# Expert weights of an attention and mixture-of-experts block loaded as bfloat16 and widened on ScalarE, with loads and zeroing cut and moved within the batch

## The chip, the cores and the metric

The kernel runs on one core of a Trainium2 chip. The metric is the device time of one launch in microseconds (us); lower is better.

## The reference

The input `x` has 8 batches of 256 tokens with 256 channels. Per batch six modulation vectors come from `silu(c) @ wmod` (`sa, ca, ga, sb, cb, gb`; the two gates are kept at least 0.25 away from zero).

```python
h = _layernorm(x) * (1 + ca) + sa
x = x + ga * attention(h)      # 32 heads of 8 channels, window of 8 keys each way
h = _layernorm(x) * (1 + cb) + sb
x = x + gb * experts(h)
```

`attention` multiplies the scores in the window by a triangular factor, takes a softmax over the window, and projects with `proj_w` and `proj_b`. `experts` sends each of the 2048 tokens to 2 of 16 experts by its sigmoid scores (float32), each expert being `(silu(h w1) * (h w3)) w2` with 176 hidden channels; a shared expert with 352 hidden channels is added for every token. The expert weights (`w1`, `w2`, `w3`, `sw1`, `sw2`, `sw3`) are bfloat16 arrays; the rest is float32.

## The kernel before, in words

The program is written engine by engine, with a semaphore for each hand-over. It has three stages.

**Stage one, attention, batch by batch.** A batch has two tiles of 128 tokens (`U` = 2). Every engine has a `main(it, first, after)` which `over(main)` calls for `it` = 0 to 7. TensorE, in the order of its own text: turn the normalised x of batch it+1 (`turn_x`), scores of the second tile (`scores(it, 1)`, L1200 and L1210), q of the next batch (`make_q`, L1172), turn the scores back (`turn_p(it, 0)`, L1219), k of the next batch (`make_k`), sums and values of the first tile (`times_v(it, 0)`, L1230 and L1237), `turn_p(it, 1)`, v of the next batch (`make_v`, L1190), the projection (`project`, L1250 and L1252), `times_v(it, 1)`, the first scores of the next batch (`scores(it + 1, 0)`), then `turn_h`, `project(it, 1)` and `gate` for the expert stage's input of the batch before. A float32 matmul has two matmul records and two weight-load records. `times_v` has 128 + 128 short records at L1237, and `scores` 64 + 64 at L1210.

ScalarE (ACT) takes the projections out of PSUM (`scaled_h` L532, `keep_q` L539, `keep_k` L546, `keep_v` L551), does the exponentials (`exponent`, L570, once per tile), and copies for the gate (`turned_h`, `gate_exp`). VectorE (DVE) masks, transposes, takes maxima off, divides by the sums, adds the residual and does both layer norms; in the last two batches it also routes the first ten tiles of tokens (`chances`, `pick`, `ranked`, `placed`). GpSimd (POOL) does the inverse roots (`rstd1`, `rstd2`) and `modulated(b)`, which writes the expert stage's input `hx` of batch b, called in `main` of batch b+1.

Transfers: q and v of each batch are spread out by DMAs. SP (SyncE) issues, per batch, `spread_q` (L352), `values_out` (v to the DRAM tensor `vd`, L358), `modulation` (the vectors of a batch, broadcast to all partitions, L372; it waits for `l2_h`), `values_in` (v back into a block pattern, rows of 256 bytes, L366; it waits for the write and for `times_v` of the batch before) and `load_x(b + 3)` (L335), in this order. `times_v(it + 1, 0)` waits for `values_in`. Everything that SP issues stays in this order.

Within this stage the weights of stage three come in, and the token table of the experts (`hslots`, 47 tiles of 128 rows, 6 MB) is zeroed. ACT issues one sixth of the zeroing (`ZEROED` = 6, 1024 KB, L589) at the end of each of its first six `main`s, and in `main(1)` also the first half of the up weights (`staged`, bfloat16, 1408 KB, L592). POOL issues the shared weights in `main(1)` (`load_shared`, L438 and L439) and the down weights `w2` in `main(2)` and `main(3)` (`load_second`, L443, two DMAs each): these go from bfloat16 in DRAM to float32 tiles in SBUF, the conversion being done by the DMA. POOL's `main` runs ahead of the others: it is in `main(1)` while TensorE is still in batch 0.

**Stage two** is the routing of the rest, and the shared expert for the first half of the tokens. POOL scatters the rows of `hx` into `hslots` (L471) once `row_z` says that the zeroing has ended. **Stage three** runs 47 tiles of rows through their experts (L1377, L1394, L1402, L1409), scatters the results (L506), and adds the rest of the shared expert and the residual.

Before all of this, ACT issues its own loads (L516 to L525) and then `scaled_h(0)` and `keep_q(0)`; half of the q spreading of batch 0 is on ACT's queue (L599). `pads` counts POOL's clearing of tiles; its seventh is after L435.

## Time and profile before

| | |
|---|---|
| median of 3 runs | 432.62 us (428.88 to 434.42) |
| the profiled execution, its own time | 430.5 us |
| its span, first to last instruction | 428.6 us |
| mean granted TensorE clock | 0.948 of full speed |
| busy: TensorE matmul, weight loads | 370.0 us (86%), 278.0 us (65%) |
| busy: VectorE | 310.4 us (72%) |
| busy: ScalarE, GpSimd | 125.5 us (29%), 124.1 us (29%) |
| moved by DMA | 52.45 MB in 53067 packets |

All rows are of that one profiled execution; times in it start at the first instruction. PE is TensorE's matmuls, PEld its weight loads, and a name with q at the end (SPq, ACTq) is an engine's issuing of DMAs. "issue" as the releaser of an idle stretch means that the profile shows no semaphore of another engine for it. The DMA share is the mean busy share of the 16 DMA engines; it is put together from packet times and can exceed 1.

### The profile page before, as it was taken

The page shows a single profiled execution, that of the slowest core. Times are in us where ns is not written, and L with a number is a line of the kernel's source. Part 1 is how long each engine was busy: PE and PEld are TensorE (multiplying, and loading weights), DVE is VectorE, ACT ScalarE, POOL GpSimd, SP SyncE. Part 2 cuts the span into 40 slices and gives each one's busy share as a digit, 9 for nine tenths or more (in the row PEclk, how much of TensorE's full clock was granted, in tenths as well). Part 3 has the DMA queues.
Part 4 walks back from the last instruction along what each step waited for, and adds up shares of the span by engine and source line. Part 5 has one row for each costly group of instructions (what it writes and reads, how often), then busy time and mean ns, then how long its engine had stood idle before and what let it go on. Part 6 is the DMA issues. An engine that isn't in the chain of part 4 may idle for free.

```text
span 428.6 us, 11940 instructions
## 1 busy us (share of the span) xinstructions
PE 370.0 (86%) x4834; PEld 278.0 (65%) x4834; DVE 310.4 (72%) x609; ACT 125.5 (29%) x301; POOL 124.1 (29%) x131
## 2 busy tenths in 40 slices
PE   6889699796999999986686958599999999999962
PEld 3568488685878888865543436477777777764452
DVE  2678578865799999999858496576666667631576
ACT  1123022311213232321023100255555555532520
POOL 6201004040030303030357586024444444440000
PEclk9999789989899999999895988899999999999988
DMA  8163905959354554425012612233333332103923
GB/s 290 54 155 107 249 21 135 263 193 227 114 125 141 106 155 106 133 71 148 2 63 98 220 62 87 77 108 104 119 120 103 114 122 72 41 3 96 297 74 122
DMA packets 53067, 52.45 MB, mean 122 GB/s; under 512 B 22148, under 2 KB 48045, under 8 KB 52406
## 3 DMA queue, kind: packets, MB, share of 16 engines
q1 hardware_dynamic: 40784, 28.68, 25.7%
q0 software_dynamic: 4528, 12.40, 9.1%
q10 hardware_dynamic: 7702, 10.62, 7.3%
q8 instruction: 39, 0.64, 0.7%
q14 instruction: 14, 0.11, 0.1%
HBM read 28.75 MB, written 20.79 MB: 116 GB/s over the span
## 4 chain that ended last, share of the span: by engine, by line
PE 65%; DVE 15%; issue 11%; DMA 2%; POOL 2%; ACT 1%; ACTq 0%; SPq 0%; DVEq 0%; POOLq 0%
PE bank L1394 10%; PE bank L1409 10%; PE bank L1283 7%; PE bank L1210 6%; PE bank L1237 6%; PE bank L1172 5%; PE bank L1346 4%; PE bank L1219 3%; PE bank L1190 3%; PE bank L1402 2%; PE bank L1377 2%; DMA first_region<-wmod 2%; DVE region L746 2%; PE bank L1252 2%; PE bank L1230 2%
## 5 line engine op out<-in xcount | busy, mean ns | idle before, releaser
L506 POOL DMA_INDIRECT yrows<-second_region,sloti x47 | 46.2, 984 | 77.0 <-ACT second_region L639 77.0
L1409 PE MATMUL bank<-w,second_region 88*128 x188 | 48.5, 380 | 0.6 <-DVE second_region L1042 0.6
L1394 PE MATMUL bank<-first_region,second_region 128*128 x141 | 42.8, 313 | 3.8 <-DVE second_region L1032 2.4
L453 POOL TENSOR_TENSOR rstd2s<-ve,cft 128x2 f32<-128x2 f32 x8 | 5.7, 708 | 137.3 <-DVE ve L793 137.3
L1283 PE MATMUL bank<-xT_region,sw 128*128 128x512 f32 (+1 forms) x96 | 45.1, 626 | 0.0
L1394 PE MATMUL bank<-region,second_region 128*128 x141 | 42.7, 312 | 0.0
L1210 PE MATMUL bank<-region,second_region 64*32 64x128 f32 x1024 | 34.5, 283 | 7.3 <-issue 7.3
L471 POOL DMA_INDIRECT hslots<-hx,posi x32 | 35.6, 1111 | 16.1 <-issue 9.0
L1210 PEld LDWEIGHTS bank<-region,second_region 64*32 64x32 f32 x1024 | 28.7, 111 | 15.6 <-issue 15.3
L1237 PE MATMUL bank<-region 128*32 128x16 f32 x2048 | 34.9, 213 | 1.8 <-issue 1.8
L1237 PEld LDWEIGHTS bank<-region 128*32 128x32 f32 x2048 | 34.9, 159 | 2.0 <-issue 2.0
L1346 PE MATMUL bank<-sw,second_region 128*128 128x256 f32 (+1 forms) x96 | 26.1, 432 | 10.2 <-DVE second_region L991 5.8
L1409 PEld LDWEIGHTS bank<-w,second_region 88*128 88x128 f32 x188 | 32.1, 190 | 4.0 <-issue 1.3
L1172 PE MATMUL bank<-second_region 128*128 128x256 f32 x128 | 32.0, 395 | 1.2 <-ACT second_region L532 1.2
L1283 PEld LDWEIGHTS bank<-xT_region,sw 128*128 128x128 f32 (+1 forms) x96 | 17.9, 191 | 22.8 <-issue 22.7
L1346 PEld LDWEIGHTS bank<-sw,second_region 128*128 128x128 f32 (+1 forms) x96 | 20.7, 220 | 16.2 <-DVE second_region L991 6.6
L746 DVE TENSOR_TENSOR region<-bank,cft 128x1024 f32<-128x1024 f32 x16 | 19.5, 1221 | 15.0 <-PE bank L1210 14.9
L769 DVE RECIPROCAL second_region<-bank 128x256 f32<-128x256 f32 x16 | 28.0, 1752 | 2.8 <-PE bank L1230 2.6
L1042 DVE COPY second_region<-bank 88x256 f32<-88x256 f32 x47 | 19.8, 420 | 12.8 <-PE bank L1402 12.7
L1037 DVE TENSOR_TENSOR second_region<-second_region,bank 128x176 f32<-128x176 f32 x47 | 15.9, 338 | 17.9 <-ACT second_region L625 17.9
L1172 PEld LDWEIGHTS bank<-second_region 128*128 128x128 f32 x128 | 23.9, 196 | 6.0 <-issue 3.2
L570 ACT ACTIVATE region<-bank 128x1024 f32<-128x1024 f32 x16 | 16.4, 1023 | 36.2 <-PE bank L1219 36.2
(163 smaller groups left out, 667.1 us busy)
## 6 DMA issues: line engine op xcount, KB each, us to landing
second_region<-hslots SPq DMA_DIRECT2D x47, 128.0 KB, 2.0
hslots<-zeros ACTq DMA_DIRECT2D x5, 1024.0 KB, 6.4
region<-vd SPq DMA_DIRECT2D x32, 128.0 KB, 5.1
region<-yrows SPq DMA_DIRECT2D x16, 256.0 KB, 6.1
modb<-moddram SPq DMA_DIRECT2D x8, 384.0 KB, 5.0
w<-w2T POOLq DMA_DIRECT2D x4, 704.0 KB, 9.1
xs<-x SPq DMA_DIRECT2D x8, 256.0 KB, 6.8
vd<-second_region SPq DMA_DIRECT2D x8, 256.0 KB, 2.2
```

Of the source, the lines that this page charges most:

```text
L471: gp.indirect_dma_start(hslots, bass.IndirectOffsetOnAxis(ap=posi[:, 0, k * TT + t:k * TT + t + 1], axis=0), hx[:, t, :], None).then_inc(r ...
L506: gp.indirect_dma_start(yrows, bass.IndirectOffsetOnAxis(ap=sloti[:, s:s + 1], axis=0), yo[:, s % RING, :], None, bounds_check=TOPK * T - ...
L746: dve.tensor_tensor(S[:, u].rearrange("p g (m t) -> p (g m) t", t=QB), SP[u][:, :].rearrange("p (m t) -> p m t", t=QB), window.unsqueeze(1 ...
L769: dve.reciprocal(rsum[:, u], SM[u]).then_inc(z_r, 1)
L1042: dve.tensor_copy(hT2[0:IH, s % 2], HT(s)).then_inc(ht_s, 1)
L1172: last = pe.matmul(o[:, c * N:(c + 1) * N], wqkv[:, k, off + c * P:off + (c + 1) * P], hT[:, k, :], start=k == 0, stop=k == C - 1)
L1210: last = pe.matmul(SPV[u][KB * o:KB * (o + 1), b // 2, :, b % 2, :], kT[OC * s:OC * (s + 1), c, q0:q0 + KB], qbd[OC * s:OC * (s + 1), c, : ...
L1237: last = pe.matmul(ZP[u][KB * r:KB * (r + 1), c, b * QB:(b + 1) * QB], vbd_h[:, BL * u + b, :, h], PT[:, u, b // 2 * 2 + h % 2, KB * (h // ...
L1283: last = pe.matmul(o[0:p], sw13[:, c, half * SI + f * P:half * SI + f * P + p], xT[:, c, g * GT * P:(g + 1) * GT * P], start=c == 0, stop= ...
L1346: last = pe.matmul(YP(i), hid_g[0:p, g % 2, f, i * P:(i + 1) * P], sw2[0:p, f, :], start=f == 0, stop=f == SK - 1)
L1394: last = pe.matmul(UP(s), parts[:, s % 2, m, c * P:(c + 1) * P], w13[c][:, bass.ds(experts[s], 1), :], start=m == c == 0, stop=m == EXACT ...
L1409: last = pe.matmul(YP(s), hT2[0:IH, s % 2, k, :], w2[:, k, bass.ds(experts[s], 1), :], start=k == 0, stop=k == 1)
```

## The change

- The shared weights and the down weights come as bfloat16, by ACT's queue, into memory that is free at the time: the rows of `hx` for batches 1 to 3 (`sw13_came`, `sw2_came`), the second half of `w2` (`w2_came[0]`) and the rows of `hx` for batches 4 to 7 (`w2_came[1]`). The first three are issued before `scaled_h(0)`, behind a wait for `pads` 7, together with the first eighth of the zeroing; the fourth is issued in `main(0)`.
- ACT widens them in 11 pieces (`piece`): two of 704 columns, one of 768, eight of 1024 columns on 88 partitions. `PIECES` gives each batch its pieces: the first stands between `scaled_h` and `keep_q`, the second between `keep_k` and `exponent(it, 1)`. Each counts `wide_s` up.
- Who writes `hx` of batch b now waits for the pieces that read it (`STAGED`), and TensorE waits for `wide_s` where it waited for the loads.
- The zeroing is in eight parts of 752 KB or less, one before the batches, and one in each of `main(0)` to `main(6)`, right behind `exponent(it, 0)`.
- `staged` is loaded in two halves, in `main(1)` and `main(2)`, behind `exponent(it, 1)`.
- On SP, `load_x(b + 3)` is issued behind `values_out(b + 1)` and ahead of `modulation(b + 1)`.
- POOL issues no weight loads any more.

```diff
-ZEROED = 6
+ZEROED = B
+PIECE = 1024
+PIECES = ((), (0, 1), (2, 3), (4, 5), (6, 7), (8, 9), (10,), ())
...
+        came = hx[:, U:].rearrange("p t d -> p (t d)").bitcast(BF16)
+        sw13_came = came[:, 0:C * 2 * SI].rearrange("p (c i) -> p c i", c=C)
+        sw2_came = came[:, C * 2 * SI:C * 2 * SI + SK * D]
+        w2_came = [w2[:, 1].rearrange("p e d -> p (e d)").bitcast(BF16)[:, 0:E * D],
+                   hx[0:IH, TT // 2:].rearrange("p t d -> p (t d)").bitcast(BF16)]
+        STAGED = {1: 3, 4: 8, 5: 9, 6: 10, 7: 11}
...
                     values_out(b + 1)
+                if b + 3 < B:
+                    load_x(b + 3)
+                if b + 1 < B:
                     modulation(b + 1)
                     values_in(b + 1)
-                if b + 3 < B:
-                    load_x(b + 3)
...
-            def load_shared():
-                gp.dma_start(sw13[:, :, :], sw13T).then_inc(ld_sw, 16)
-                gp.dma_start(sw2[:, :, :], sw2T).then_inc(ld_sw, 16)
-            def load_second(k):
-                for e in range(0, E, E // 2):
-                    gp.dma_start(w2[:, k, e:e + E // 2, :], w2T[:, k, e:e + E // 2, :]).then_inc(ld_w2, 16)
...
                 wait(gp, mod_ld, 16 * (b + 1))
+                if b in STAGED:
+                    gp.wait_ge(wide_s, STAGED[b])
...
+            def zero(k):
+                a, z = k * NS // ZEROED, (k + 1) * NS // ZEROED
+                act.dma_start(hslots_t[:, a:z], zeros[:, :].unsqueeze(1).to_broadcast([P, z - a, D])).then_inc(row_z, 16)
+            def load_second(k):
+                act.dma_start(w2_came[k], w2T[:, k].rearrange("p e d -> p (e d)")).then_inc(ld_w2[k], 16)
+            def load_first(k):
+                n = STAGE // 2
+                act.dma_start(staged[:, k * n:(k + 1) * n], w13T[:, k * n:(k + 1) * n]).then_inc(ld_ew, 16)
+            def piece(i):
+                if i < C:
+                    act.wait_ge(ld_sw, 32)
+                    last = act.activation(sw13[:, i], sw13_came[:, i], ACT.Copy)
+                elif i == C:
+                    last = act.activation(sw2[:, :, :].rearrange("p f d -> p (f d)"), sw2_came, ACT.Copy)
+                else:
+                    k, j = divmod(i - C - 1, E * D // PIECE)
+                    act.wait_ge(ld_w2[k], 16)
+                    at = slice(j * PIECE, (j + 1) * PIECE)
+                    if k == 1:
+                        act.wait_ge(wide_s, C + 1 + E * D // PIECE)
+                    last = act.activation(w2[:, k].rearrange("p e d -> p (e d)")[:, at], w2_came[k][:, at], ACT.Copy)
+                last.then_inc(wide_s, 1)
             def main(it, first, after):
                 if after:
                     scaled_h(it + 1)
+                if PIECES[it]:
+                    piece(PIECES[it][0])
+                if after:
                     keep_q(it + 1)
                 exponent(it, 0)
+                if it == 0:
+                    load_second(1)
+                if it + 1 < ZEROED:
+                    zero(it + 1)
                 if after:
                     keep_k(it + 1)
+                for i in PIECES[it][1:]:
+                    piece(i)
                 exponent(it, 1)
+                if it == 1:
+                    act.wait_ge(mod_p, 3)
+                if it in (1, 2):
+                    load_first(it - 1)
                 if after:
                     keep_v(it + 1)
...
+            act.wait_ge(pads, 7)
+            act.dma_start(sw13_came, sw13T).then_inc(ld_sw, 16)
+            act.dma_start(sw2_came, sw2T.rearrange("p f d -> p (f d)")).then_inc(ld_sw, 16)
+            load_second(0)
+            zero(0)
             scaled_h(0)
             keep_q(0)
```

## Rows read from the trace of the kernel before

**Rows 1.** The page's first part: busy time of each engine.

```profile
PE 370.0 (86%) x4834; PEld 278.0 (65%) x4834; DVE 310.4 (72%) x609; ACT 125.5 (29%) x301; POOL 124.1 (29%) x131
```

**Rows 2.** Chain that ended last, whole span: start, length, what.

```profile
129.68 1.88 PE bank L1210 x64
...
151.22 1.88 PE bank L1210 x64
```

**Rows 3.** The same chain from 38 to 130 us, small pieces too.

```profile
45.06 2.91 issue
...
52.42 3.57 PE bank L1210 x64
...
63.51 0.29 issue
...
82.18 1.35 issue
...
84.52 1.19 issue
...
94.91 0.65 issue
...
102.81 3.76 issue
...
108.42 3.00 PE bank L1172 x8
...
123.68 0.61 issue
```

**Rows 4.** Windows from the span's start: length, busy (xrecords) by engine, clock, DMA.

```profile
0.00:45.06 45.06, 38.19 (x601) 27.27 (x602) 28.59 (x60) 9.06 (x14) 12.31 (x21) 1.00 0.52 158
0.00:61.00 61.00, 50.35 (x734) 36.34 (x736) 38.99 (x70) 12.14 (x19) 12.31 (x21) 0.94 0.54 152
0.00:63.60 63.60, 52.87 (x855) 38.70 (x856) 41.27 (x73) 12.30 (x19) 12.31 (x21) 0.95 0.52 147
...
0.00:102.85 102.85, 88.40 (x1616) 68.35 (x1617) 73.02 (x125) 21.51 (x36) 22.63 (x33) 0.95 0.63 168
```

**Rows 5.** Windows of busy DMA; the last three figures are clock, DMA share, GB/s.

```profile
40.00:54.00 14.00, 10.22 (x255) 7.51 (x257) 9.04 (x12) 1.02 (x2) 1.49 (x3) 0.83 1.00 251
72.00:90.00 18.00, 15.31 (x273) 13.21 (x266) 14.33 (x20) 4.62 (x9) 0.71 (x1) 0.91 1.10 280
98.00:109.50 11.50, 7.60 (x106) 5.78 (x99) 6.59 (x7) 1.88 (x5) 0.00 (x0) 0.90 1.17 252
124.00:132.00 8.00, 7.59 (x146) 6.30 (x146) 7.29 (x9) 1.88 (x5) 0.00 (x0) 1.00 1.00 254
```

**Rows 6.** A window of 2 us in which only large pieces move.

```profile
84.00:86.00 2.00, 0.81 (x54) 0.77 (x46) 1.76 (x1) 0.00 (x0) 0.00 (x0) 1.00 1.09 409
```

**Rows 7.** Timeline of DMA issues: start, length, engine, line, what.

```profile
39.40 0.41 ACTq L589 DMA_DIRECT2D hslots<-zeros  x1
...
40.12 0.78 POOL L438 DMA_DIRECT2D sw<-sw13T  x1
...
69.88 3.25 SPq L366 DMA_DIRECT2D region<-vd  x4
```

**Rows 8.** Timeline of ACT within batch 4; in brackets its idle time before.

```profile
133.52 0.60 ACT L539 ACTIVATE second_region<-bank 128x512 f32<-128x512 f32 x1 [3.49 <-PE bank L1172]
...
139.67 1.02 ACT L570 ACTIVATE region<-bank 128x1024 f32<-128x1024 f32 x1 [2.95 <-PE bank L1219]
```

**Rows 9.** Timeline of the start.

```profile
12.35 0.12 POOL L435 MEMSET apart<- 128x16 f32 x1
...
15.44 1.02 ACT L532 ACTIVATE second_region<-bank,modT 128x256 f32<-128x256 f32 x2 [11.65 <-PE bank L1164]
```

**Rows 10.** Windows of the start and of the change from batch 6 to 7.

```profile
12.00:20.00 8.00, 6.80 (x30) 4.05 (x29) 5.81 (x19) 1.61 (x3) 1.18 (x7) 1.00 0.03 8
...
190.00:212.00 22.00, 14.01 (x387) 11.75 (x383) 20.36 (x37) 2.90 (x5) 1.50 (x2) 0.94 0.35 92
```

More of the change, by code:

```diff
@@ L277, in build @@
         xT_p, xT_s, lg_p, lg_s = (sem(n) for n in ("xT_p", "xT_s", "lg_p", "lg_s"))
-        ld_g, ld_sw, ld_w2, ld_ew, ld_late = (sem(n) for n in ("ld_g", "ld_sw", "ld_w2", "ld_ew", "ld_late"))
+        ld_g, ld_sw, ld_ew, ld_late = (sem(n) for n in ("ld_g", "ld_sw", "ld_ew", "ld_late"))
         su_p, su_s, su_m, sy_p, sy_s, sh_s = (sem("s" + n) for n in ("u_p", "u_s", "u_m", "y_p", "y_s", "h_s"))
@@ L283, in build @@
         row_z = sem("row_z")
+        wide_s = sem("wide_s")
+        ld_w2 = [sem(f"ld_w2{k}") for k in range(2)]
         val_s, slot_p, who_s, exp_s = (sem(n) for n in ("val_s", "slot_p", "who_s", "exp_s"))
@@ L474, in main @@
             def main(it, first, after):
-                if it == 1:
-                    load_shared()
-                elif it in (2, 3):
-                    load_second(it - 2)
                 if not first:
@@ L584, in main @@
                     gate_exp(it - 1)
-                if it == 0:
-                    act.wait_ge(pads, 7)
-                if it < ZEROED:
-                    a, z = it * NS // ZEROED, (it + 1) * NS // ZEROED
-                    act.dma_start(hslots_t[:, a:z], zeros[:, :].unsqueeze(1).to_broadcast([P, z - a, D])).then_inc(row_z, 16)
-                if it == 1:
-                    act.wait_ge(mod_p, 3)
-                    act.dma_start(staged, w13T[:, 0:STAGE]).then_inc(ld_ew, 16)
+            act.wait_ge(pads, 7)
[3 more added lines that the diff above has]
+            zero(0)
             scaled_h(0)
@@ L909, in modulated @@
                 dve.wait_ge(mod_ld, 16 * (b + 1))
+                dve.wait_ge(wide_s, STAGED[b])
                 dve.tensor_tensor(h2[:, :, :], h2[:, :, :],
@@ L1322, in main @@
                 if not after:
-                    pe.wait_ge(ld_sw, 32)
+                    pe.wait_ge(wide_s, C + 1)
                     pe.wait_ge(ga_s, TT - 1)
@@ L1413, in _ @@
             pe.wait_ge(su_m, SK * AHEAD)
-            pe.wait_ge(ld_ew, 16)
+            pe.wait_ge(ld_ew, 32)
             pe.wait_ge(ld_late, 16)
-            pe.wait_ge(ld_w2, 64)
+            pe.wait_ge(wide_s, 11)
             pe.wait_ge(exp_s, 1)
```

## The prediction

> **What bounds the kernel now.** I read the page's busy times first: TensorE's matmuls are 86% of the span and no other engine passes 72% [rows 1]. So the end is set by TensorE and by whatever stops it. The chain that ended last tells what stops it. Where nothing does, a batch of the attention takes 151.22 - 129.68 = 21.54 us from one run of second scores to the next [rows 2]. The three batches before that took 129.68 - 52.42 = 77.26 us [rows 2, 3], which is 12.6 us over 3 x 21.54.
>
> The small pieces of the chain show where it goes: seven stretches called "issue", of 2.91, 0.29, 1.35, 1.19, 0.65, 3.76 and 0.61 us, together 10.8 us [rows 3]. The stretches of 2.91 and 3.76 us lie in the middle of 64 matmuls of one loop, which have no semaphore between them, so no other engine's work is awaited. Counting records shows what is. Up to the first stretch TensorE has 601 + 602 = 1203 of them, up to the second 855 + 856 = 1711, up to that at 102.81 us 1616 + 1617 = 3233 [rows 4]. The distances are 508 = 2 x 254 and 1522 = 6 x 253.7. I read this as blocks of about 254 visible instructions, fetched from memory while the block before them is run; TensorE stands when the next one isn't there.
>
> The Trainium skill, Runtime: NRT & Kernel Launch, section "Instruction fetch mechanics", says that a program is streamed in blocks of 16 KiB, 256 instructions, by a DMA queue of the sequencer's own, while the current one runs, and that crossing a boundary is mostly hidden. The block agrees with the distances above, the hiding does not agree with 3.76 us. By its rule that crossings cost next to nothing these pieces would have another cause and the time would stay; that is a rival below.
>
> How long a fetch takes can be seen twice. With the DMA engines nearly idle, the block that begins just before 61.0 us (734 + 736 = 1470 records, 13 beyond an edge at 1457) [rows 4] is run through by 63.51 us and its successor is there at 63.80 [rows 3]: about 2.9 us. With 14 us of DMA at share 1.00 around it the gap at 45.06 lasts to 47.97, and in the 11.5 us at 1.17 the one at 102.81 lasts to 106.57 [rows 3, 5]. A batch with 8 us at 1.00, from 124 to 132 us [rows 5], has 0.61 us at its beginning, and none of any size later. So what costs is the long stretches. They are long where POOL's converting weight loads meet the zeroing and the values, as at 39.40 and 40.12 us [rows 7], or the load of 1408 KB in batch 1.
>
> The stretch of 1.35 us at 82.18 us is another thing: it stands before `times_v`, which waits for the values that SP issued from 69.88 to 73.13 us [rows 7]. I take it for their late landing, in the stretch 72 to 90 us [rows 5].
>
> After the longer gaps the clock is granted at 1.2 instead of 2.4 GHz for a while: 64 score matmuls take 3.57 us, against 1.88 [rows 2, 3], and the mean clock of the stretch 40 to 54 is 0.83 [rows 5]. All of it beside the gaps is about 12.6 - 7.9 = 4.7 us in batches 1 to 3 (7.85 being the six gaps behind 52.42 us), of which some 0.3 is waiting in the normal order; I take 4.4 us for the clock in all.
>
> **The change part by part.** The sum is made against the profiled execution, 430.5 us, of which the span is 428.6; the median of the runs is 432.6, 2.1 us higher.
>
> *What is removed.* Everything above: gaps of 10.8 us and slow clock of 4.4 us, together 15.2 us, if no stretch of busy DMA stays long. The weights now need half the bytes at their destination, none is converted on the way, and none meets the end of a batch except half of the up weights. POOL loses its issues (0.78 us for one [rows 7]), hidden before and after.
>
> *What is added to the middle of each batch.* Behind `exponent(it, 0)` come 752 KB of zeroing. At the 0.4 MB/us of a window with large pieces [rows 6] this is 1.9 us; in batch 0, with the fourth load of 704 KB, 3.7 us. Just then TensorE comes to `times_v`, 256 records in 2.1 us, where it needs a block in hardly more than the 2.9 us that a fetch takes unhindered. A batch has 972 records (2 x 132 for scores, 2 x 288 for `times_v`, 48 for q, k and v, 84 for the rest), 3.8 blocks, so the edges move through it by some 45 records a batch, and only some batches fall badly. Two short blocks matter. The one around `times_v(it, 0)` falls badly in batch 1 (the gap of 0.29 us): its fetch would be asked for at 61 us, with the zeroing of that batch just begun. The one around `times_v(it, 1)` and the next scores falls badly in batches 0, 2, 3 and 4: there the write of v, the load of x (256 KB, now ahead of the modulation, 0.6 us) and in batch 2 half of the up weights (704 KB, 1.8 us) are before it, in batch 0 also the modulation (384 KB, 1.0 us).
>
> How much of such a backlog a fetch waits for is not in the trace as such. Bounds: none of it, as the gaps of 0.29 to 0.65 us without load show; or all of it. The gap at 45.06 lies between: of 1024 + 704 KB and more issued before it, at 0.4 MB/us over 4.3 us, it saw some 3.3 beyond 2.9. I take three quarters. That gives 0.9 us in batch 0, 0.3 + 1.4 in batch 1, 0.6 + 1.2 in batch 2, 0.6 + 0.4 in batch 3, 0.1 in batch 4: 5.5 us that stay. With none of it 1.6 us stay (0.29 + 0.65 + 0.61), with all of it 7.3. Gaps under 2 us I take to leave the clock alone, as the one of 0.61 did.
>
> *ACT's pieces.* Each first piece stands before `keep_q`, where ACT was idle for 3.49 us, each second one before `exponent(it, 1)`, with 2.95 us [rows 8]. A copy of 1024 columns isn't shown; the nearest row is an exponential of 1024 columns out of PSUM, 1.02 us [rows 8]. Between 0.6 us (512 columns) and twice 1.02 us everything fits into those idle stretches, so I take 0 for all eleven. Were the cover gone, each would cost its 1 us. TensorE's `make_q` runs while the first piece does, so `keep_q` isn't late. Each issue of a DMA on ACT, 0.4 to 0.6 us [rows 7], comes where ACT waits for TensorE anyway (0.7 us or more); I take 0, at most 0.2 each where two meet. The waits for `wide_s` in POOL are met one batch ahead, save that for batch 1, where the third piece comes at the start of batch 2 and the use in its second half.
>
> *The start.* ACT waits for the seventh `pads` at 12.47 us and issues four DMAs, some 2 us, and then has `scaled_h(0)`, for which it sat until 15.44 us [rows 9]. So 1 us is left. The four carry 2.0 MB, 5 us of DMA, into 8 us where the share was 0.03 [rows 10]; ACT's half of the q spreading at 19.3 us comes behind them. They should be through at 18 us. I take 0.3 us; bounds 0 and 2.
>
> *The order on SP.* `load_x` was held up behind the values, and no one waited for it; ahead of `modulation` it puts 0.6 us in front of modulation and values, which have 5 us or more to spare. 0 us beyond the share taken above.
>
> *What is late next.* From the sixth batch on VectorE is busy for 20.4 of 22 us [rows 10]; its work there starts when TensorE lets it and moves forward whole. The expert stage and the zeroing's end (last part near 180 us, awaited by the scatter behind 212) are not on the path.
>
> Sum: 430.5 - 15.2 + 5.5 + 0.3 = 421.1; I round to 421.
>
> **The rivals.**
> - *All stretches short enough.* If a fetch waits for hardly any backlog, 1.6 us stay in place of 5.5: 417 us. For it: 8 us at share 1.00 brought no gap inside the stretch. Against it: batches 0 to 3 had their edges elsewhere.
> - *Middle and end both hurt.* The 752 KB hit every `times_v(it, 0)`, and gaps of 1.5 to 2 us come in six batches, with the clock once or twice: 11 us stay, 427 us. For it: the blocks there are the fastest. Against: in most batches the edge lies outside them.
> - *The middle becomes worse than the end was.* One mechanism: the fetch asked for in `times_v` waits for the whole backlog in all seven batches that have one (3 us each), TensorE stands long enough for the lower clock each time (1 us), 28 us in place of 15.2: 443 us. It decides from 2.2 us a batch. Against it, the same as above, and that 1.9 us of zeroing can hardly cost 3.
> - *The gaps aren't due to transfers.* Then they stay, and the time with them: 430.5 us. Against it: all large ones lie in the stretches of [rows 5].
>
> **How the numbers follow.** Forecast 0.48, all short 0.22, both hurt 0.19, worse than before 0.05, no connection 0.06. The range takes in the first three with the start's bound: 413 to 430. A difference of 2%, 8.7 us, is about what a measurement of this kernel can tell; the border is at 424.0. Faster by over 2%: nearly all of the first two, some of the third, 0.69. Within 2%: 0.26. Slower by over 2%: 0.05.
>
> **What would show it.** In the profile after: seven batches of 21.5 to 23.5 us; no "issue" piece over 2 us in the chain before 190 us, and those that are left at multiples of 254 records, in or right behind `times_v`; no window of 8 us with a DMA share over 1; a granted clock of 1.00 until 190 us. The forecast is wrong if batch 1 to 3 still take 25 us, if gaps sit in the middle of each batch, if `scaled_h(0)` or the first scores come over 1 us later than before, or if ACT's pieces take over 2 us and `exponent(it, 1)` moves.

## The result, and the profile after

| | before | after |
|---|---|---|
| median of 20 runs each | 433.11 us (428.88 to 436.73) | 429.41 us (425.67 to 434.93) |
| ratio, 95% interval | | 0.9915 (0.9887 to 0.9943) |
| the profiled execution, its own time | 430.5 us | 427.58 us |
| its span, clock | 428.6 us, 0.948 | 425.6 us, 0.944 |

The kernel became faster by 3.7 us, where 9.4 were forecast: the right side, inside the range, but well under half of the size, and not more than the 2% by which the text counts a kernel as faster. A kernel's runs can fall into a faster and a slower group; the ratios compare the faster runs alone, the medians are of all runs.

One figure of the change differs from what is said above. The zeroing goes in whole tiles of 128 KB, so its eight parts are 640 KB (the first) and 768 KB (the others), not 752 KB. In the kernel before, the first of the six parts is 896 KB and the others are 1024 KB.

The page of the kernel after, busy time of each engine:

```profile
PE 371.0 (87%) x4834; PEld 278.0 (65%) x4834; DVE 310.1 (73%) x609; ACT 135.0 (32%) x312; POOL 120.7 (28%) x125
```

TensorE's busy time is that of [rows 1]. ACT has 11 instructions and 9.5 us more, which are the pieces; POOL has 6 instructions less. So the work is as described, and the question is again where TensorE stands.

The chain that ended last, kernel after, from 38 to 140 us (start, length, what):

```profile
46.92 0.40 issue
...
51.36 1.88 PE bank L1253 x64
...
60.76 1.91 issue
62.67 0.71 PE bank L1262 x5
63.38 3.02 PE bank L1233 x8
...
66.61 1.16 PE bank L1295 x4
...
76.33 1.88 PE bank L1253 x64
...
91.39 1.20 issue
...
99.05 1.88 PE bank L1253 x64
...
115.12 0.44 issue
...
120.95 1.88 PE bank L1253 x64
...
137.66 0.62 issue
```

Five gaps are left, 0.40 + 1.91 + 1.20 + 0.44 + 0.62 = 4.6 us, where [rows 3] had seven with 10.8 us. From one run of second scores to the next the batches take 25.0, 22.7 and 21.9 us. Batch 1 is the bad one: the gap of 1.91 us splits eight transposes (L1262) into 3 and 5, and behind it the values of the next batch (`make_v`, L1233) take 3.02 us in place of the 1.73 us of the other batches, the projection (L1295) 1.16 in place of 0.86.

Windows of the kernel after (length, busy by engine with records, then clock, DMA share and GB/s); the first three end at gaps:

```profile
0.00:46.92 46.92, 40.19 (x601) 27.77 (x602) 28.76 (x60) 9.06 (x14) 11.00 (x19) 0.96 0.76 215
0.00:60.76 60.76, 52.13 (x855) 37.62 (x856) 41.27 (x73) 13.66 (x21) 11.00 (x19) 0.97 0.68 190
0.00:137.66 137.66, 125.07 (x2506) 98.74 (x2507) 108.12 (x179) 37.88 (x59) 27.29 (x35) 0.98 0.56 155
64.00:66.00 2.00, 2.00 (x6) 1.50 (x5) 0.00 (x0) 0.44 (x1) 1.92 (x2) 0.50 0.73 189
12.00:14.00 2.00, 2.00 (x8) 0.68 (x7) 0.70 (x3) 0.00 (x0) 1.23 (x7) 0.62 0.36 59
```

The first two gaps stand at exactly the records of [rows 4], 601 + 602 and 855 + 856, although the times and everything that the DMAs do there have changed. The last is at 5013 records, 3810 behind the first, 15 x 254. So a gap looks like a block of the program that hasn't come.

The trace shows the block itself. The page's list of DMA queues (packets, MB, share of the 16 engines) has one for instructions:

```profile
q8 instruction: 39, 0.64, 0.6%
```

Each of these 39 packets is of 16384 bytes, and the trace keeps the time of each, though no view prints it. At the gap of 60.76 us the packet runs from 60.18 to 61.06 us, and TensorE goes on at 62.67. At the longest gap of the kernel before it runs from 103.82 to 105.06 us, and TensorE goes on at 106.57. In all 20 profiles of this case the attention has 76 gaps of over 0.25 us at such an edge, and every one ends 0.9 to 1.6 us after the end of such a packet. What waits behind the data is the packet: in `weights_only`, an experiment below that has no burst ahead of this edge, it starts as TensorE enters the block before (57.62 and 57.74 us), in the kernel after 2.0 us later (60.18 and 58.17 us). One gap of the kernel before is of another kind: that at 82.18 us stands at 2388 records, at no edge, before `times_v`.

The rest of the time lies outside the attention's middle. From the first scores (24.17 us before, 26.03 after, in TensorE's timeline) to the second scores of batch 5 (151.14 and 143.08 us) the kernel after gains 9.9 us. Of this it has 2.9 us left at the end. The timeline of TensorE, kernel after, at the start and at the change from batch 6 to 7 (start, length, line, count, idle before):

```profile
11.12 2.30 PE L1189 MATMUL bank<-first_region,cts 128*8 128x512 f32 x4 [2.06 <-DMA first_region<-wmod]
...
190.14 3.50 PE L1253 MATMUL bank<-region,second_region 64*32 64x128 f32 x64
```

The start loses 1.9 us before the first scores, and here the new transfers have no part in it. TensorE waits 2.06 us for `wmod` where it waited 1.63 us, and that wait is over at 11.12 us, before ACT issues its first load of the change (12.54 us); from then on the clock is 0.62 in the window from 12 us. For the spreading of q it waits no longer than before (1.57 and 1.63 us). The profiles of the same kernel and of the kernel before on another chip run the start at full speed. The scores of the last batch take 3.50 us at 1.2 GHz (1.95 in the profile before, but 3.64 in a second profile of the kernel before), which I don't put down to the change either. The clock is down some instructions earlier already, so from the scores before to the end of these the kernel after takes 13.5 us and the kernel before 10.8: 2.7 us. The third piece is new. VectorE and ScalarE, kernel after, timeline of stage two, idle time and its releaser in brackets:

```profile
235.91 0.69 DVE L1030 TENSOR_TENSOR second_region<-second_region,bank 128x512 f32<-128x512 f32 x1 [2.75 <-issue]
239.62 0.26 DVE L881 TENSOR_TENSOR score<-bank,have 128x96 f32<-128x96 f32 x1 [3.02 <-remote]
...
239.71 0.60 ACT L651 ACTIVATE second_region<-bank 128x512 f32<-128x512 f32 x1 [3.83 <-PE bank L1326]
```

The second ranking (`ranked`, L881) follows the line before it in 0.6 us in the kernel before; here it comes 3.02 us late. What it reads from TensorE was written at 235.5 us, and ACT goes on at the same moment. The profile names "remote", on a program of one core, so nothing that it knows. This one lies on the path: the scatter's indices and the tiles' experts come out of this ranking.

### The profile page after: what moved, and what is told of

It reads as the page before. It is cut to its first block, busy times and chain, and to the rows that moved or that the text cites. A ratio compares the mean times of both kernels' runs of the same rounds, so it can differ in the third digit from the quotient of the medians.

```text
span 425.6 us, 11956 instructions
## 1 busy us (share of the span) xinstructions
PE 371.0 (87%) x4834; PEld 278.0 (65%) x4834; DVE 310.1 (73%) x609; ACT 135.0 (32%) x312; POOL 120.7 (28%) x125
## 2 busy tenths in 40 slices
DMA packets 52993, 50.45 MB, mean 119 GB/s; under 512 B 22122, under 2 KB 48147, under 8 KB 52636
## 3 DMA queue, kind: packets, MB, share of 16 engines
q1 hardware_dynamic: 40784, 28.68, 24.5%
## 4 chain that ended last, share of the span: by engine, by line
PE 62%; DVE 17%; issue 12%; DMA 3%; POOL 2%; ACT 1%; another core or an unknown queue 1%; ACTq 0%; SPq 0%; DVEq 0%; POOLq 0%
PE bank L1437 10%; PE bank L1452 10%; PE bank L1280 6%; PE bank L1215 5%; PE bank L1253 5%; PE bank L1326 5%; PE bank L1389 4%; PE bank L1262 3%; PE bank L1233 3%; PE bank L1445 2%; PE bank L1420 2%; DMA first_region<-wmod 2%; DVE region L788 2%; PE bank L1295 2%; PE bank L1273 2%
## 5 line engine op out<-in xcount | busy, mean ns | idle before, releaser
L1253 PE MATMUL bank<-region,second_region 64*32 64x128 f32 x1024 | 33.6, 279 | 1.5 <-issue 1.5
L1326 PEld LDWEIGHTS bank<-xT_region,sw 128*128 128x128 f32 (+1 forms) x96 | 17.9, 191 | 22.8 <-issue 22.7
L1215 PE MATMUL bank<-second_region 128*128 128x256 f32 x128 | 30.9, 385 | 1.2 <-ACT second_region L537 1.2
L672 ACT ACTIVATE second_region<-bank 128x256 bf16<-128x256 f32 x47 | 18.0, 383 | 29.4 <-PE bank L1420 29.3
```

The source lines that it names most:

```text
L672: act.activation(parts[:, s % 2, 0], RTP(s), ACT.Copy).then_inc(hi_s, 1)
L1215: last = pe.matmul(o[:, c * N:(c + 1) * N], wqkv[:, k, off + c * P:off + (c + 1) * P], hT[:, k, :], start=k == 0, stop=k == C - 1)
L1253: last = pe.matmul(SPV[u][KB * o:KB * (o + 1), b // 2, :, b % 2, :], kT[OC * s:OC * (s + 1), c, q0:q0 + KB], qbd[OC * s:OC * (s + 1), c, : ...
L1326: last = pe.matmul(o[0:p], sw13[:, c, half * SI + f * P:half * SI + f * P + p], xT[:, c, g * GT * P:(g + 1) * GT * P], start=c == 0, stop= ...
```

## The experiments

Eighteen kernels ran in five groups, four of them repeats. Each group ran on one chip, and its kernels share the runs of the kernel before; ratios are to those, with their 95% intervals, and times are compared within a group first.

**First group: the kernel itself again, and two of its parts.**

> The changed kernel once more, to see which pieces of its profile come back. Theory A (what the attention gains is given back behind it, by the program itself): the wait of 3.0 us before the second ranking (L881) and the slow clock between batches 6 and 7 (64 score matmuls in 3.5 us) are there again, and the scatter of the first round starts about 6 us earlier than before. Theory B (the losses behind the attention are chance of one execution): at least one of the two is gone and the execution is 2 to 5 us shorter. Both expect gaps of 4 to 6 us in the attention in place of 10.8.

> The kernel before once more. Theory A: no wait before its second ranking, full clock between batches 6 and 7, gaps of 9 to 12 us in the attention. Theory B: the gaps of the attention are there, and one of the two losses behind it may show here as well.

424.77 us against 429.32 before, 0.9909 (0.9868 to 0.995): the result repeats. The profile has gaps of 1.64, 0.94, 0.44 and 0.61 us and no wait at L881. The second profile of the kernel before, 429.53 us, has gaps of 2.36, 2.54, 0.98, 1.13, 3.29 and 0.70 us, 11.0 in all; the largest is again in the second scores of batch 3 (102.18 us), and the one of 2.54 us, at 78.95 us, is new in size. It stands before `times_v`, as that of 82.18 us did.

`late_load` moves the late up weights (`w13_late`, into the memory of the first modulation weights) behind more of ACT's work:

```diff
+            for n in range(3, SK * AHEAD - 1):
+                silu_g(n)
             act.wait_ge(z_p, TT)
             act.dma_start(w13_late, w13T[:, STAGE:]).then_inc(ld_late, 16)
-            for n in range(3, SK * AHEAD):
-                silu_g(n)
+            silu_g(SK * AHEAD - 1)
```

> The late half of the up weights (w13_late, 1408 KB) is issued behind the fifth silu of the shared expert instead of behind the third, some 7 to 10 us later. If the wait of 3.0 us before L881 is an instruction block of VectorE held up by this load, it goes, and the time is 2 to 3 us under the changed kernel's (ratio to before about 0.985), unless the load holds up another block in its new place. If the wait has another cause, it stays and the time with it (0.991).

423.14 us, 0.9907 (0.9865 to 0.9949), the same as `after_again`. On this chip neither kernel has the wait, so it says nothing of it. The two profiles differ in one thing that matters below: behind nearly the same gap in batch 1, 1.64 and 1.65 us, `after_again` has `make_v` at 2.64 us, a slow clock, and `late_load` at 1.73, full speed.

`zero_end` leaves the first part of the zeroing where it is and takes the seven others from the middle of the batches to their ends:

```diff
-                if it + 1 < ZEROED:
-                    zero(it + 1)
...
                     gate_exp(it - 1)
+                if it + 1 < ZEROED:
+                    zero(it + 1)
```

> The changed kernel with the eight parts of the zeroing (but the first) put back to the end of each batch. If the burst in mid-batch causes the gap of 1.91 us in batch 1 behind times_v, that gap falls to about 0.3 us; the gaps at the end of batches 2 to 4 grow or stay. Theory that placement matters: the attention changes by more than 2 us, ratio 0.98 or 1.0. Theory that only size and conversion matter: within 1 us of the changed kernel, 0.99.

423.07 us, 0.9893 (0.9829 to 0.9956). Batch 1's gap is down to 0.26 us; one of 1.55 us is in batch 0. By time alone the kernel can't be told from `after_again` (1.7 us less) or `late_load` (0.1 us less), the interval being 1.3% wide, but the gap went when the burst left the middle.

**Second group: one part of the change alone.** `weights_only` is the kernel before with the weights as bfloat16, ACT's pieces and the waits for them; the zeroing stays in six parts at the ends of batches, the up weights are issued together in batch 1, SP's order is the old one. `zero_only` is the kernel before with the eight parts (one ahead, seven mid-batch), `x_only` has only `load_x` moved. `x_undone` is the kernel after with SP's old order:

```diff
-                if b + 3 < B:
-                    load_x(b + 3)
-                if b + 1 < B:
                     modulation(b + 1)
                     values_in(b + 1)
+                if b + 3 < B:
+                    load_x(b + 3)
```

> The kernel before with only the weights changed: bfloat16 by ACT's queue into free memory and widened by ACT; zeroing in six parts at the ends of batches, the up weights in one stretch in batch 1, and SP's order, all as before. Theory C (the long stretches came from the converting loads): the gaps of 2.9 and 3.8 us at the ends of batches 0 and 2 shrink below 1.5 us, those of batch 1 (up weights and zeroing together) stay; attention 5 us shorter than before, the ratio 0.993. Rival (size of the zeroing parts decides): attention less than 2 us shorter, ratio 1.0.

> The kernel before with only the zeroing changed: eight parts, the first ahead of the batches, the others behind the first exponential of batches 0 to 6. Theory C: the gaps at the ends of batches 0 and 2 stay above 2 us because the converting loads are there, and batch 1 gains a gap of 1.5 us behind times_v; ratio 0.997 to 1.003. Rival (size of the zeroing decides): attention 5 us or more shorter, ratio 0.993.

> The kernel before with only SP's order changed (load of x ahead of modulation and values). All theories: no gap goes, within 1 us of before, ratio 1.00. If the load of x in front of a block asked for in times_v costs what I took (0.4 to 0.9 us in batches 0 and 2 to 4), the attention is 0.5 to 2 us longer.

> The changed kernel with SP's order put back. If the load of x costs the gaps of batches 2 to 4, they shrink by 0.3 us each and the ratio to before is 0.989; if it frees the values, ratio 0.993. I expect no difference that can be measured: 0.991.

| kernel | median, us | ratio to before (429.19 us) |
|---|---|---|
| `weights_only` | 418.51 | 0.9746 (0.9674 to 0.9818) |
| `zero_only` | 430.68 | 1.0037 (0.998 to 1.0095) |
| `x_only` | 430.27 | 1.0011 (0.9969 to 1.0052) |
| `x_undone` | 423.39 | 0.9888 (0.9816 to 0.9961) |

The weights alone give 10.7 us, where the whole change gave 3.7 above and, without SP's order (`x_undone`), 5.8 us here. That is far more than the 0.993 expected: the gaps put down to batch 1's loads were to stay and went too. (The gap at 45 us, on the other hand, stays above the 1.5 us expected.) The other two parts alone can't be told from nothing (1.5 and 1.1 us over the kernel before, with 1.0 inside both intervals). The chain of `weights_only` from 38 to 140 us has two gaps left of the seven:

```profile
45.07 1.82 issue
...
110.19 0.41 issue
```

And that of `zero_only`, same stretch, has six, of which five are shown (the last is 0.32 us):

```profile
44.92 2.89 issue
...
61.26 1.91 issue
...
77.09 1.40 issue
...
84.96 1.27 issue
...
107.68 1.67 issue
```

The reader is to see three things. With the converting loads on POOL's queue the gap at 45 us (2.9) stays wherever the zeroing is. The largest gap of [rows 3], 3.76 us at 102.81 us and 3233 records, is not there: these scores run through. What stands at 107.68 us is at 3360 records, at no edge, and so is that at 84.96; both are before `times_v`, of the kind of the gap at 82.18 us in [rows 3]. So moving the zeroing took away a gap of the end of batch 2 that was expected to stay, and gained others, and the time can't be told from that of the kernel before. And a gap of 1.91 us at 61.26 us appears that is only 0.29 us in [rows 3]: it is the kernel after's gap at 60.76 us, made by the zeroing in the middle of batch 1 without any help of the weights.

**Third group: each small part on top of `weights_only`.** `w_zero_mid` has the eight parts of the zeroing as in the kernel after; `w_zero_start` has the first of the six parts ahead of the batches and the others at their ends; `w_halves` has the up weights in halves behind `exponent(it, 1)`; `w_x` has SP's new order.

```diff
-                if it < ZEROED:
+                if 0 < it < ZEROED:
                     zero(it)
...
             load_second(0)
+            zero(0)
             scaled_h(0)
```

> weights_only (ratio 0.9746) with the zeroing of the change added: eight parts, the first ahead of the batches, the others in mid-batch. Theory D (the zeroing's place and cut give back what the weights gain): first scores 0.5 us later, a gap of 1 to 2 us behind times_v in batch 1, and in the medians most of the 5 to 6 us between weights_only and the changed kernel: ratio 0.985 to 0.99. Rival (the other edits do it): ratio 0.975 to 0.98.

> weights_only with the first of its six zeroing parts (1024 KB) ahead of the batches in place of the end of batch 0. If the backlog at the end of batch 0 makes the gap of 1.8 us at 45 us, it falls below 0.5 us; the q spreading of ACT's queue lands 0.5 to 1 us later. Both together: within 1 us of weights_only, ratio 0.973 to 0.977. If what stands at the start costs more than the profile shows, 0.98 or more.

> weights_only with the up weights in two halves, in batches 1 and 2 behind the second exponential. Theory D: no difference, 0.975. Rival (the half in front of the write of v delays a block in batch 2, and the values): a gap of 1 to 2 us in batch 2, ratio 0.98 or more.

> weights_only with the load of x ahead of modulation and values on SP. Theory D: no difference that can be measured, 0.975 to 0.977. Rival: 0.5 to 1 us more of gaps in batches 2 to 4, 0.98.

| kernel | median, us | ratio to before (434.31 us) |
|---|---|---|
| `w_zero_mid` | 427.58 | 0.9876 (0.9821 to 0.993) |
| `w_zero_start` | 424.06 | 0.9783 (0.9718 to 0.9847) |
| `w_halves` | 423.02 | 0.9786 (0.9727 to 0.9846) |
| `w_x` | 423.18 | 0.976 (0.9699 to 0.9821) |

SP's order and the halves have ratios that can't be told from `weights_only`'s. Nor can that of the part ahead of the batches: the runs of `w_zero_start` go from 422.18 to 429.60 us, those of `w_x` from 421.70 to 428.61. Its own expectation missed in two places, the gap at the end of batch 0 being 1.32 us and not under 0.5, and the q spreading over 2 us late. The zeroing in the middle costs 3.5 us against `w_zero_start` and 4.4 against `w_x`. (The part moved by `w_zero_start` is 896 KB, not 1024.) How the start can lose is in the timeline of TensorE; first `w_x`, nothing of the zeroing ahead:

```profile
23.29 0.59 PE L1242 MATMUL bank<-cbt 128*128 128x512 bf16 x2 [1.62 <-DMA region<-second_region]
23.81 1.95 PE L1252 MATMUL bank<-region,second_region 64*32 64x128 f32 x64
```

then `w_zero_mid`:

```profile
25.53 0.62 PE L1242 MATMUL bank<-cbt 128*128 128x512 bf16 x2 [3.69 <-DMA region<-second_region]
26.09 3.53 PE L1252 MATMUL bank<-region,second_region 64*32 64x128 f32 x64
```

TensorE waits for the spreading of q, which is behind 1.9 MB of weights and zeroing, for 3.69 in place of 1.62 us, and then has the scores at half the clock. Both kernels issue that spreading at nearly the same time (19.1 us in `w_zero_mid`, 18.9 in `w_x`). On this chip `w_zero_start` waits for 3.88 us too; the kernels of the first two groups with the same loads ahead wait for 2.0 to 2.5 us.

Batch 1 of `w_zero_mid` has the gap in the middle and no slow clock behind it:

```profile
63.33 1.90 issue
65.23 0.71 PE bank L1261 x5
65.94 1.73 PE bank L1232 x8
```

All four profiles of this group have the wait at the second ranking, 2.3 to 3.0 us.

**Fourth group: no part ahead of the batches, and the load behind the fifth silu.** `no_start_part` is the kernel after with seven parts, in the middle of batches 0 to 6; they are larger, 896 KB in batch 1. `weights_again` is `weights_only` unchanged; `w_late` is it with the edit of `late_load`; `before_third` is the kernel before.

```diff
-ZEROED = B
+ZEROED = B - 1
...
-                if it + 1 < ZEROED:
-                    zero(it + 1)
+                if it < ZEROED:
+                    zero(it)
...
             load_second(0)
-            zero(0)
             scaled_h(0)
```

> The changed kernel with seven zeroing parts, one in the middle of each of batches 0 to 6, and none ahead of the batches. Theory E (the start costs 1 to 4 us, the mid-batch parts the rest): q spreading of batch 0 lands in 1.9 us, first scores at 24.0 us and not later, the gap of 1.6 to 1.9 us in batch 1 stays; ratio 0.980 to 0.986, between weights_only (0.975) and the changed kernel (0.991). If the ratio is that of weights_only, the start was all of it; if that of the changed kernel, the middle is.

> weights_only once more: ratio 0.972 to 0.980. If this chip is one where the wait before the second ranking shows, it is there (2 to 3 us) and the ratio is at the upper end.

> weights_only with the late up weights issued behind the fifth silu of the shared expert. If the load holds up VectorE before the second ranking on this chip, weights_again has the wait and this kernel has none there, and is 2 to 3 us shorter unless the load holds up something behind it; if weights_again has no such wait, both are the same within 0.5%.

> The kernel before: if the wait before the second ranking comes from the load and the chip alone, it shows here as soon as weights_again shows it; if it needs the changed program, it does not.

| kernel | median, us | ratio to before (432.75 us) |
|---|---|---|
| `no_start_part` | 428.77 | 0.9984 (0.9942 to 1.0026) |
| `weights_again` | 423.04 | 0.9847 (0.9785 to 0.9909) |
| `w_late` | 423.32 | 0.9855 (0.9792 to 0.9917) |
| `before_third` | 432.04 | one run |

`no_start_part` was a miss: without the part ahead the first scores are back at 24.16 us, and batch 0 has no gap over 0.2 us any more, yet the kernel isn't better. Chain of waits of `no_start_part`:

```profile
49.25 1.88 PE bank L1252 x64
...
58.66 2.19 issue
60.86 1.23 PE bank L1261 x5
62.08 2.79 PE bank L1232 x8
```

and of `weights_again`, with the zeroing at the ends:

```profile
50.61 1.88 PE bank L1251 x64
...
60.02 0.01 issue
60.03 0.71 PE bank L1260 x5
60.73 1.73 PE bank L1231 x8
```

The block edge is in the same place in both, between the third and the fourth of eight transposes. With 896 KB in front of it it costs 2.19 us, and 0.5 + 1.1 us more by the slow clock in the next two lines; without, 0.01 us. So `no_start_part` takes 25.2 us for batch 1 and `weights_again` 21.4.

The wait of the ranking is longest here, 3.75 us in the chain of `weights_again`:

```profile
228.52 3.75 another core or an unknown queue
...
232.30 0.27 DVE score L879
```

The same kernel in the second group has nothing there:

```profile
229.62 0.69 DVE second_region L1028
230.31 0.18 DVE score L879
```

`w_late` was to take it away if the load issued at that time made it; it has 3.79 us. That explanation is out. `before_third` is the one profile of the kernel before in a group where the wait shows. VectorE's ranking (L839) follows at once there, but ACT's timeline has the same stall at the same place:

```profile
245.93 0.60 ACT L609 ACTIVATE second_region<-bank 128x512 f32<-128x512 f32 x1 [4.67 <-remote]
```

ACT comes 1.5 us late (4.67 us idle, against 3.15 in the other two profiles of the kernel before), while VectorE ranks beside it, and ACT has no long wait behind it. So in these executions something stops ACT here in either kernel; with the new weights it stops VectorE too, ahead of the ranking, and that is on the path. What it is stays open.

**Fifth group: is it the middle, or batch 1?** `middle_but_one` is `no_start_part` with only batch 1's part moved to the end of its batch. `w_zero0_mid` is `weights_only` with only batch 0's part moved from the end to the middle.

```diff
-                if it < ZEROED:
+                if it < ZEROED and it != 1:
                     zero(it)
...
                     gate_exp(it - 1)
+                if it == 1:
+                    zero(1)
```

> The kernel no_start_part (the changed kernel with its seven zeroing parts in the middle of batches 0 to 6 and none ahead of the batches) with batch 1's part alone moved to the end of batch 1. If what the middle of batch 1 costs is its gap and the slow clock behind it, batch 1 falls from 25.2 to about 21.8 us between second score groups, and the kernel is about 3.5 us under no_start_part: a ratio to the kernel before near 0.990. If the placement in every later batch costs as much, it stays within 1 us of no_start_part, near 0.998.

> The kernel weights_only with its first zeroing part (1024 KB) in the middle of batch 0, not at its end; the others stay at the ends of batches. If the middle is free in batch 0, the gap of 1.8 us at about 45 us goes, batch 0 falls from 23.75 to about 22.1 us and the kernel is 1.6 us under weights_again: a ratio near 0.98. If a burst in the middle of a batch costs wherever it is put, batch 0 has a new gap of about 2 us and the ratio stays at 0.985 or above.

| kernel | median, us | ratio to before (429.07 us) |
|---|---|---|
| `middle_but_one` | 420.21 | 0.9805 (0.9763 to 0.9847) |
| `w_zero0_mid` | 418.29 | 0.9756 (0.9715 to 0.9796) |

Chain of `middle_but_one`:

```profile
49.05 1.88 PE bank L1254 x64
...
57.99 1.02 PE bank L1263 x8
59.02 1.73 PE bank L1234 x8
...
70.45 1.88 PE bank L1254 x64
```

The eight transposes are whole, the clock stays, batch 1 takes 21.4 us. Windows of DMA of the two kernels where the block is fetched, first `no_start_part`, then `middle_but_one`:

```profile
56.00:58.00 2.00, 2.00 (x139) 2.00 (x128) 1.99 (x2) 0.97 (x2) 0.00 (x0) 1.00 1.03 321
58.00:60.00 2.00, 0.66 (x15) 0.51 (x12) 1.68 (x8) 0.00 (x0) 0.05 (x1) 1.00 0.25 73
```

```profile
56.00:58.00 2.00, 2.00 (x133) 1.97 (x124) 1.85 (x2) 0.78 (x2) 0.00 (x0) 1.00 0.15 45
58.00:60.00 2.00, 2.00 (x14) 1.87 (x15) 1.81 (x8) 0.95 (x1) 0.23 (x1) 1.00 0.21 61
```

Two microseconds of DMA at share 1.03 right before the edge make it late. The single packets say so too: the one of this block starts at 58.47 us in `no_start_part`, 2.4 us after TensorE entered the block before (56.07), and at 55.75 in `middle_but_one`, where that block is entered at 55.87 us. The parts in the middle of the six other batches leave no gap over 0.7 us but one of 1.48 us in batch 2, at full clock. The kernel stands at 0.9805, better than the expected 0.990. The 1.8% between it and `no_start_part` are 7.7 us: 3.8 are batch 1, and 3.8 are the wait at the ranking, which this chip doesn't have (the ranking follows at once, at 228.42 us). That the second half is the chip's doing, and not the edit's, is argued from the groups and not shown.

`w_zero0_mid` was a miss as to batch 0: moving 896 KB of zeroing (not 1024) out of the way of the gap left 1.58 us of 1.80. The block's packet still starts 2.7 us after the block before is entered; in `middle_but_one`, where the gap is gone, it is 1.4 us. Taken over all profiles, batch 0's gap is gone (0 to 0.5 us) only where the zeroing is in the middle and `load_x` is ahead of the values too (`after`, `after_again`, `late_load`, `no_start_part`, `middle_but_one`); with either alone it is 1.3 to 1.8 us (`x_undone` and `w_zero_mid`; `w_x` and `zero_end`). Why, stays open. The kernel is at 0.9756, level with `weights_only`; these two are the best of the case, and `w_zero0_mid` is the only one whose whole interval lies below 0.98. Both lie some 2.5% under the kernel before (`weights_again`, with the wait, 1.5%), where the changed kernel lies 0.9% under it, and in their own groups `weights_only` is 4.9 us under `x_undone`, `w_zero0_mid` 1.9 us under `middle_but_one`.

## Why the prediction was right or wrong

*What was removed* was right. The gaps lay at the block edges foreseen. Of the seven, the three at 82.18, 84.52 and 102.81 us went and that at 45.06 us fell to 0.40 us, and from the first scores to batch 5 the profile gained 9.9 us where 9.7 were forecast. Which part of the change removes them wasn't asked: the forecast put the removal down to the change as a whole. The weights alone do all of it and more: this stretch takes 127.0 us in the kernel before (124.6 and 124.7 in its other two profiles, so some 2 us of the 9.9 are that execution's), 117.1 in the kernel after and 113.3 in `weights_only`. Here a rule speaks to the reason. The Trainium skill, DMA: Bandwidth & Descriptors, section "Issuing engines are not separate DMA queues", says that transfers issued by any engine end up on the same 16 DMA engines and interleave there. By it, ACT's queue in place of POOL's gives nothing by itself. No run changes the queue alone: the weights part moves 50.45 in place of 52.45 MB, moves 1.2 MB of it into the start, and ends the conversion on the way, all at once, and which of these counts stays open.

*That a fetch waits behind other transfers* was right as well. The prediction took 2.9 us for a fetch without load; the packet of that fetch runs from 60.82 to 62.25 us, and TensorE goes on at 63.80. How much of a backlog a fetch waits for "is not in the trace as such", it said; the packets do show it, and that of the gap at 45.06 us starts 4.1 us after the block before is entered.

*What stays*, 5.5 us, came out at 4.6 us of gaps. Batch by batch, 0 to 4, the forecast was 0.9, 1.7, 1.8, 1.0 and 0.1 us, and 0.40, 1.91, 1.20, 0.44 and 0.62 were measured. The gap in the middle of batch 1 was nearly right in place and size (0.3 + 1.4 us; 1.64 to 2.19 us in the other profiles with the zeroing there).

*"Gaps under 2 us I take to leave the clock alone"* failed. Behind 1.91 us the window at 64 us has a clock of 0.50, and about 1.7 us go in three lines, for which the sum had nothing. With it the mid-batch part of batch 1 costs 3.6 us (`no_start_part`: 3.8), against nothing at the batch's end. But the length of a gap doesn't decide it: `w_zero_mid`, `x_undone` and `late_load` have gaps of 1.90, 1.64 and 1.65 us in the same place and keep the clock. `middle_but_one`, without this part and without the part ahead of the batches, comes to 0.9805; the forecast was 421.1 / 430.5 = 0.978.

*The start*, 0.3 us with bounds 0 and 2. "They should be through at 18 us" failed: in the kernel after the DMA share is still 0.74 in the window from 18 to 20 us. What that costs differs: TensorE's wait for the spreading of q grows by 0.4 to 0.9 us in four profiles and not at all in the profiled execution, whose 1.9 us lie before it. In `w_zero_mid` it grows by 2.1 us, beyond the bound, and with the clock the first scores end 3.9 us later than in `w_x` (29.62 against 25.76 us). In the medians of the third group the part ahead doesn't show. Weights and zeroing together do it, neither does alone: `zero_only` and `w_x` have their first scores at 24.03 and 23.81 us.

*"Moves forward whole"* is the step that failed most in the profiled execution, with a term of nothing for what comes behind the attention. Of 9.9 us gained, 2.9 arrive. The start takes 1.9, the slow clock around 190 us 2.7 and the wait at the second ranking 3.0; the rest gives 0.6 back. The first two vary from execution to execution of either kernel. The third is in none of the three profiles of the kernel before, nor in `zero_only` and `x_only`, and in 8 of 15 with the new weights, in all of the third and the fourth group. None of the forecast's terms or rivals had it. That it takes the new weights and certain chips is likely but rests on little: only the fourth group has a profile of the kernel before beside it. In the first group, without this wait, the step held: the second scores of batch 5 start 7.9 us earlier in `after_again` than in `before_again` (140.63 and 148.50 us), and the span is 7.4 us shorter (420.3 and 427.7). The medians of that group are only 4.6 us apart, so what a middling execution loses beyond these profiles stays open.

*ACT's pieces and SP's order* at 0 us: nothing speaks against it. `weights_only` has all 11 pieces and is one of the two best; `x_only` is at 1.0011, `w_x` equals `w_halves` within the noise. *The expert stage* wasn't late.

Of the prediction's own signs of being wrong, one came in part, batch 1 alone of the three taking 25 us, and one in full, the first scores being 1.9 us late. The second didn't come back in the other profile of this kernel (24.56 against 23.88 us in `before_again`), the first did (24.5 us). Of the rivals, "both hurt" (427 us) is where the time lies, but its mechanism isn't what happened: not six batches, one. "The gaps aren't due to transfers" is refuted by `weights_only` and by the packets.

## What to carry to other kernels

Run the parts of a change apart: here one of four gave 10.7 us, and the zeroing's new places took back 4 to 5 us in the second and third groups (in the first, `zero_end` can't be told from the kernel with the zeroing in the middle). Where TensorE stands inside a loop without a semaphore, count records for the block edges, and look at the packets of the instruction queue. In these traces the fetch goes out at the earliest when the block before is entered, so keep bursts of DMA from the few microseconds ahead of that moment, above all where that block is run through in some 3 us; here a burst cut smaller and moved there was worse than a larger one at the batch's end. A gap may also cost twice its length: the one of 1.91 us took another 1.7 us by the clock, though one of 1.90 us took nothing more.

## What the runs showed of the hardware that wasn't expected

- TensorE's program comes over the DMA engines in packets of 16 KB, one for about 254 records, and the packet starts at the earliest as the block before is entered (57.62 and 57.74 us in `weights_only`). TensorE goes on 0.9 to 1.6 us after the packet's end (76 gaps in 20 profiles), and at the gap of 45.06 us of the kernel before the packet starts 4.1 us after that moment.
- A block edge is at the same record, 601 + 602 and 855 + 856, in kernels whose timing around it differs, and with no burst ahead of it costs 0.01 us.
- The length of a gap alone doesn't tell whether the clock falls behind it. In the middle of batch 1, `make_v` takes 3.02 us behind 1.91 us (`after`), 1.73 behind 1.90 (`w_zero_mid`), 2.64 behind 1.64 (`after_again`) and 1.73 behind 1.64 (`x_undone`). At the end of batch 0 the next 64 scores take 3.57 us behind 2.91 (`before`), while `zero_only` keeps the full clock behind 2.89.
- 1.9 MB issued from 12.5 to 14.2 us still hold up the transfers issued from 19 us on (TensorE waits 2.0 to 3.9 us for them in six profiles, but 1.57 in `after`); the same without the zeroing (`w_x`) don't (1.62 us).
- VectorE stands for 2.3 to 3.8 us ahead of the second ranking, and ACT goes on in the same moment, in kernels with the new weights on some chips and not on others, and no semaphore is named; in the kernel before only ACT does, in one of three profiles. The late load of the up weights is excluded as its cause. A block of VectorE's or ScalarE's own instructions that comes late wasn't tried. The trace has a second instruction queue, q14, and none of its packets falls into the wait (214.84 and 249.43 us are the nearest in `after`), but which engines it serves isn't shown.
